# Quantised cross attention: totals and clips on GpSimd, two V roundings on VectorE, weights scaled one row tile later, value products in two visits

## The reference, cut to what matters

```
def _fq(x, delta, zp, n_bits):
    xi = _round_ste(x / delta) + zp
    xq = jnp.clip(xi, 0.0, 2.0 ** n_bits - 1.0)
    return (xq - zp) * delta

k = (ctx @ wk).reshape(b, m, H, DH).transpose(0, 2, 1, 3)
v = (ctx @ wv).reshape(b, m, H, DH).transpose(0, 2, 1, 3)
sim = einsum('bhid,bhjd->bhij', _fq(q, dq, 128.0, 8), _fq(k, dk, 128.0, 8)) * SCALE
attn = softmax(sim, axis=-1)
out = einsum('bhij,bhjd->bhid', _fq(attn, dw, 0.0, 8), _fq(v, dv, 128.0, 8))
```

## Time and profile before

| what | value |
|---|---|
| median of 3 runs | 2426.47 us (2419.76 to 2426.48) |
| the profiled execution | 2418.64 us, of which the span is 2417.0 us |
| mean granted TensorE clock | 0.907 |
| busy share of the span | TensorE 82%, VectorE 71%, ScalarE 56%, GpSimd 29% |
| this stage in the trace | 1675 to 2352 us |

### The profile page before, as it was taken

How to read it: one execution, slowest core, us unless ns; L and a number is a source line. 1 busy time by engine, 2 the same in 40 slices (tenths; PEclk the granted TensorE clock), 3 DMA queues, 4 the chain that set the end, 5 groups by cost and what they waited for, 6 DMA issues and landing times. The chain is left out here.

```text
span 2417.0 us, 58085 instructions
## 1 busy us (share of the span) xinstructions
PE 1986.4 (82%) x19941; PEld 1285.8 (53%) x19941; DVE 1709.3 (71%) x3300; ACT 1360.2 (56%) x2415; POOL 694.8 (29%) x510
## 2 busy tenths in 40 slices
PE   3778677599999999999887785445988888888888
PEld 3778243266666666666534452222555555555553
DVE  3556496677777777777523326995899999999984
ACT  2544243266666666666533333222888888888862
POOL 0000161111111111111000002331766666666630
PEclk8999798799999999999988897556999999999999
DMA  7888000223323323233009980000111111111100
GB/s 193 228 237 222 5 1 0 77 71 91 91 68 95 84 75 95 79 80 95 20 38 280 270 228 1 0 0 26 42 40 35 38 38 38 38 38 38 38 1 15
DMA packets 108285, 190.36 MB, mean 79 GB/s; under 512 B 19886, under 2 KB 75294, under 8 KB 108222
## 3 DMA queue, kind: packets, MB, share of 16 engines
q1 hardware_dynamic: 103614, 164.95, 25.2%
q0 software_dynamic: 4608, 24.58, 3.1%
HBM read 127.13 MB, written 25.49 MB: 63 GB/s over the span
## 5 line engine op out<-in xcount | busy, mean ns | idle before, releaser
L1217 DVE TENSOR_REDUCE c_part<-c_mxp 128x1 f32<-128x500 f32 x672 | 429.4, 674 | 173.7 <-PE c_mxp L1106 169.3
L1190 ACT ACTIVATE c_e<-c_stp 125x896 f32<-125x896 f32 x384 | 351.9, 917 | 97.1 <-PE c_stp L1118 96.5
L1854 ACT ACTIVATE c_e<-c_sp,alpha 128x750 f32<-128x750 f32 x448 | 392.7, 882 | 23.6 <-PE c_sp L1798 21.4
L1812 PE MATMUL c_tp<-ident_h,c_ph 128*128 128x128 f16 x2688 | 230.5, 223 | 72.7 <-DVE c_pt L1874 70.8
L1812 PEld LDWEIGHTS c_tp<-ident_h,c_ph 128*128 128x128 f16 x2688 | 181.1, 100 | 167.7 <-DVE c_pt L1874 113.5
L1106 PE MATMUL c_mxp<-c_kh,c_qb 128*128 128x500 f16 x672 | 254.2, 380 | 3.1 <-DVE c_part L1217 2.2
L1874 DVE TENSOR_SCALAR c_pt<-c_tp 125x768 bf16<-125x768 f16 x448 | 246.3, 550 | 3.5 <-PE c_tp L1812 2.2
L1768 POOL TENSOR_SCALAR c_ki<-c_clipped 128x500 bf16<-128x500 bf16 x96 | 193.0, 2010 | 150.6 <-DVE c_clipped L1885 138.3
L1060 POOL TENSOR_TENSOR c_qs<-qst,mask_quad_ 96x224 f16<-96x224 f32 (+1 forms) x128 | 67.5, 556 | 578.1 <-PE c_stp L1118 578.1
L1133 PE MATMUL c_pvp<-c_e,c_vx 125*32 125x168 f32 (+1 forms) x6144 | 227.0, 265 | 0.6 <-ACT c_e L1190 0.4
L1918 DVE TENSOR_SCALAR c_ph<-c_e,c_inv 128x1500 f16<-128x1500 f32 x224 | 224.1, 1000 | 4.3
(11 more groups left out here) (267 smaller groups left out, 3452.9 us busy)
## 6 DMA issues: line engine op xcount, KB each, us to landing
c_ct<-ctx_turned SPq DMA_DIRECT2D x64, 750.0 KB
ctx_turned<-l_ct POOLq DMA_DIRECT2D x32, 750.0 KB, 4.7
c_ks<-c_kh SPq DMA_DIRECT2D x256, 93.8 KB
f_ct<-ctx_turned SPq DMA_DIRECT2D x32, 750.0 KB
l_cn<-in_ctx SPq DMA_DIRECT2D x32, 672.0 KB
f_cn<-in_ctx SPq DMA_DIRECT2D x32, 672.0 KB
c_ks<-c_kl SPq DMA_DIRECT2D x128, 93.8 KB
l_cn<-in_ctx SPq DMA_DIRECT2D x32, 78.0 KB
```

Of the source, the lines that this page charges most:

```text
L1190: act.activation(e[:, j % 4, :].rearrange("p (a c) -> p a c", a=2), stp[0:KP, 2 * (j % 2):2 * (j % 2) + 2, 0:448], ACT.Exp, scale=SCALE).t ...
L1217: dve.reduce_max(part[:, s // 3, s % 3:s % 3 + 1], mxp[:, (PIECES * p + s) % 2, 0:500], axis=AX.X).then_inc(piece_max, 1)
L1812: last = pe.transpose(tp[:, h, 128 * k:128 * k + 128], ph[r][:, KP * j:KP * j + 128], m.ident_h[:, :])
L1854: act.activation(e[r][:, HALF * h:HALF * h + HALF].rearrange("p (k c) -> p k c", k=2), sp_[:, 2 * h:2 * h + 2, 0:375], ACT.Exp, scale=m.al ...
```

## The change

GpSimd takes the totals, one column per row tile, and the whole clip: first to the limits with ROUND still in the number, in f32 (c_clamped), then ROUND taken off, into bf16. VectorE rounds the pieces 4 and 5 of V from PSUM (ON_VECTOR); ScalarE keeps the other four. VectorE makes the weights of row tile t - 1 in slot t. There are four buffers c_e instead of two, and c_half, c_total and c_inv have a column per row tile. Projections stand in the slots 0, 1, 2, 4, 5, 6 (PROJECT), and the value products in two visits of six steps, in slots 3 and 5 (WEIGH). The turn on TensorE and the copies on VectorE stay in their slots. The diff, cut to its core:

```diff
-        WEIGH = [0, 2, 5, 7, 9, NJ]
+        PROJECT = (0, 1, 2, 4, 5, 6)
+        WEIGH = {3: (0, 6), 5: (6, NJ)}
+        E_BUFFERS = 4
+        ON_VECTOR = (4, 5)
+        USED_BACK = [4 if t >= E_BUFFERS else NT if t == 3 else 3 for t in range(NT)]
-        clipped = pair("clipped", [128, 512], BF16)
+        clamped = pair("clamped", [128, 512])
-        e = pair("e", [128, NK])
+        e = [sb(f"e{t}", [128, NK]) for t in range(E_BUFFERS)]
-        half = sb("half", [128, 2, 2])
-        total, inv = sb("total", [128, 1]), sb("inv", [128, 1])
+        half = sb("half", [128, NT, 2])
+        total, inv = sb("total", [128, NT]), sb("inv", [128, NT])
...
+                def clip(n, p, k, live):
+                    i = 6 * n + k
+                    rows, width = (128, 500) if k < 3 else (KP, 512)
+                    if k >= 2 or live(1):
+                        pool.wait_ge(proj_ready, i - 1)
+                    wait_apart(pool, proj_rounded, i + 1, beat)
+                    pool.tensor_scalar(clamped[k % 2][0:rows, 0:width], rounded[k % 2][0:rows, 0:width],
+                                       ROUND + 127.0, ROUND - 128.0, ALU.min, ALU.max).then_inc(proj_clamped, 1)
...
+                    wait_apart(pool, proj_clamped, i + 1, beat)
+                    pool.tensor_scalar(out, clamped[k % 2][0:rows, 0:width], -ROUND, 1.0, ALU.add, ALU.mult
+                                       ).then_inc(proj_ready, 1)
...
-                        pool.tensor_scalar(out, clipped[t % 2][0:rows, 0:width], -128.0, None, ALU.max
-                                           ).then_inc(proj_ready, 1)
-                sweep(pool, step, 0)
+                    for t in range(NT):
+                        if live(1):
+                            i = NT * (n - 1) + t
+                            wait_apart(pool, exped, 2 * i + 2, beat)
+                            pool.tensor_scalar(total[:, t:t + 1], half[:, t, 0:1], half[:, t, 1:2], m.delta[:, 7:8],
+                                               ALU.add, ALU.mult).then_inc(totalled, 1)
+                        if live(0) and t in PROJECT:
+                            clip(n, p, PROJECT.index(t), live)
+                sweep(pool, step, 1)
...
-                        if 2 <= t and live(2):
-                            for j in range(WEIGH[t - 2], WEIGH[t - 1]):
+                        if t in WEIGH and live(2):
+                            for j in range(*WEIGH[t]):
...
+                            i = NT * (n - 1) + t
+                            if t >= E_BUFFERS or live(2):
+                                act.wait_ge(p_ready, i - USED_BACK[t] + 1)
...
+                def invert(a, t):
+                    i = NT * a + t
+                    dve.wait_ge(totalled, i + 1)
+                    dve.reciprocal(inv[:, t:t + 1], total[:, t:t + 1]).then_inc(inverted, 1)
+
+                def weights(a, t, r, first):
+                    i = NT * a + t
+                    dve.wait_ge(inverted, i + 1)
+                    if t >= 2 or not first:
+                        dve.wait_ge(p_turned, 2 * (i - 1))
+                    dve.tensor_scalar(ph[r][:, 0:NK], e[t % E_BUFFERS][:, :], inv[:, t:t + 1], HALF_ROUND,
+                                      ALU.mult, ALU.add).then_inc(p_ready, 1)
...
+                        if t == 0:
+                            made = live(2)
+                            item = (n - 2, NT - 1)
+                            r, first = (NT * p + NT - 1) % 2, not live(3)
+                        else:
+                            made = live(1)
+                            item = (n - 1, t - 1)
+                            r, first = (NT * (1 - p) + t - 1) % 2, not live(2)
...
+                            if h == 0 and made:
+                                invert(*item)
+                        if made:
+                            weights(*item, r, first)
+                        if live(0) and t in PROJECT and PROJECT.index(t) in ON_VECTOR:
+                            k = PROJECT.index(t)
+                            i = 6 * n + k
+                            dve.wait_ge(proj_done, i + 1)
+                            dve.wait_ge(proj_clamped, i - 1)
+                            dve.tensor_scalar(rounded[k % 2][0:KP, :], pp[0:KP, 0:512], m.rdelta[0:KP, 6:7],
+                                              ROUND, ALU.mult, ALU.add).then_inc(proj_rounded, 1)
```

More of the change, by code:

```diff
@@ L1770, in _ @@
-                sweep(pool, step, 0)
+                def clip(n, p, k, live):
[6 more added lines that the diff above has]
+                                       ROUND + 127.0, ROUND - 128.0, ALU.min, ALU.max).then_inc(proj_clamped, 1)
+                    if k < 3 and live(2):
+                        pool.wait_ge(s_done, 2 * NT * (n - 1))
+                    if k >= 3 and live(2):
+                        pool.wait_ge(weighed, NJ * (n - 2) + 4 * (k - 2))
+                    wait_apart(pool, proj_clamped, i + 1, beat)
+                    out = (ki[p][:, 500 * k:500 * k + 500] if k < 3 else
+                           vi[p][:, 4 * (k - 3):4 * (k - 3) + 4, :].rearrange("p j c -> p (j c)"))
+                    pool.tensor_scalar(out, clamped[k % 2][0:rows, 0:width], -ROUND, 1.0, ALU.add, ALU.mult
+                                       ).then_inc(proj_ready, 1)
@@ L1848, in step @@
                         if live(1):
-                            a, r = n - 1, (NT * (1 - p) + t) % 2
-                            if t >= 2 or live(2):
-                                act.wait_ge(p_ready, NT * a + t - 1)
+                            i = NT * (n - 1) + t
+                            if t >= E_BUFFERS or live(2):
+                                act.wait_ge(p_ready, i - USED_BACK[t] + 1)
                             for h in range(2):
-                                act.wait_ge(s_done, 2 * NT * a + 2 * t + h + 1)
-                                act.activation(e[r][:, HALF * h:HALF * h + HALF].rearrange("p (k c) -> p k c", k=2),
+                                act.wait_ge(s_done, 2 * i + h + 1)
+                                act.activation(e[t % E_BUFFERS][:, HALF * h:HALF * h + HALF]
+                                               .rearrange("p (k c) -> p k c", k=2),
                                                sp_[:, 2 * h:2 * h + 2, 0:375], ACT.Exp, scale=m.alpha[:, 1:2],
-                                               accum_out=half[:, r, h:h + 1]).then_inc(exped, 1)
-                        if live(0) and t < 6:
-                            i = 6 * n + t
+                                               accum_out=half[:, t, h:h + 1]).then_inc(exped, 1)
+                        if live(0) and t in PROJECT and PROJECT.index(t) not in ON_VECTOR:
+                            k = PROJECT.index(t)
+                            i = 6 * n + k
                             act.wait_ge(proj_done, i + 1)
[L1860 to L1863, removed]
+                            if k >= 2 or live(1):
+                                act.wait_ge(proj_clamped, i - 1)
+                            rows, width, d = (128, 500, 5) if k < 3 else (KP, 512, 6)
+                            act.activation(rounded[k % 2][0:rows, 0:width], pp[0:rows, 0:width], ACT.Identity,
                                            bias=m.round[0:rows, 0:1], scale=m.rdelta[0:rows, d:d + 1]
```

45 lines of the change are left out of this document (13 added, 32 removed).

## The result

The changed kernel takes 2485.5 us (median of 4 runs, 2482.5 to 2495.3) against 2423.1 for the kernel before (4 runs): ratio 1.0265, 95% interval 1.023 to 1.030, so 62 us slower. Its profiled execution took 2482.5 with a span of 2480.9, 64 more than the span before. The stage now runs from 1675 to 2415 us, 740 instead of 677: all of the difference lies in it.

What follows compares the result with a forecast made beforehand. VectorE ends last now; after the change, the c_ph-turn-copy chain and GpSimd's exclusion bound it. 11.4 + 2.76 + 3.22 + 4.92 = 22.3, or 20.8; middle 21.5, plus 0.5: 22.0 per item, +47 us, 2468; range 2405 to 2605.

Steps and rivals of the forecast that it cites:

- the main case: Whole kernel: the change makes it slower, 2468 us within 2440 to 2510; chance 0.42.
- The chain: From c_ph over TensorE's turn and VectorE's copies to the next c_ph: 2.76 us a slot, bounds 2.6 and 2.9.
- VectorE's work: Per item VectorE loses 7 totals (2.2) and 6 clips (1.9), gains 2 V roundings (1.2): net -2.9 us.
- GpSimd's pass: c, one clip pass of 500 columns on GpSimd: 0.80 us, ends 0.51 and 1.45; two passes per piece.
- The slot behind slot 5: After VectorE's rounding, GpSimd's passes run from 0.57 to 2.23 and c_ph ends at 3.22 us.
- The boundary: Between items: c_ph ends at 4.92 us if behind GpSimd's c_qb, 3.40 if in front; the middle taken.
- The lower clock: 0.5 us per item above the clean sum, kept from the present item: TensorE waits at the boundary, granted clock 0.92.
- The totals: On GpSimd, one column, 0.17 us each; 1 to 1.5 us of queue hidden while c is below about 1.
- Rival A: GpSimd's pass costs what its present clip does, c = 1.45: 26.3 us an item, 2605 us; chance 0.25.
- Rival B: The chain holds but c_qb falls into a gap: 20.7 us an item, no change, 2430 us; chance 0.10.
- Rival C: As B, with c_total and c_ph not blocked at the boundary and no lower clock: 2414 us; chance 0.15.
- Rival D: Turn and copy never wait for the newest c_ph, TensorE's work decides: 18.4 us an item, 2361 us; chance 0.08.

Runs made afterwards that it cites:

- Opening the chain: Changed kernel with TensorE's turn and VectorE's copies also one slot later (row tile t - 3 in slot t): 2356.6 us, ratio 0.971 to the kernel before.
- form experiment: Changed kernel with the six pieces clipped on GpSimd in six different forms of operations and types, to price them: 2610.6 us, a single execution.

## Why the prediction was right

Forecast 2468, measured 2485.5, inside the 2440 to 2510 of the main case; slower, by 45 forecast and 62 measured. The mechanism is the forecast's: the chain sets the slots and the collision lengthens the boundary. Of its signs, VectorE's busy share fell to 0.80 as it says, and TensorE waits for c_ph; VectorE's wait for turned halves is 135 us where it says 60 to 110, and c_ph's mean 1160 ns where it says 1200 or more. By its own steps:

- The chain. Forecast 2.76 a slot; measured 2.80, and 2.79 in the slot shown above. The one guess in it, the wake-up of 0.04, measured 0.03; the start of the turn came 0.13 after c_ph, not 0.10. Opening the chain gave 129 us, so it is shown as a cause, not only seen.
- VectorE's work. Forecast -2.9 us an item; its busy time fell by 39 us, 1.2 an item, of which the held c_ph take back 1.0 (256.8 us for all c_ph against 224.1 before). A V rounding lasts 0.74 where I took 0.67. The work fell, and did not decide.
- GpSimd's pass. I took c = 0.80 between 0.51 and 1.45; it is 0.61. So the passes do not set the slots after ScalarE's roundings: 2.80, which is the chain, instead of 2.85. To interpolate between a write and c_qb was the wrong way to a price: the form experiment shows neighbours at 0.61, 1.47 and 1.93. It was luck that 0.80 fell near, and the error had a price at the boundary.
- The slot behind slot 5. Forecast 3.22, held by passes; measured 3.06 from c_ph's end to c_ph's end (2002.79 to 2005.85). With two steps of the value products instead of six in slot 5 a pass held c_ph to the same 3.06, so two limits lie together here.
- The boundary. I put c_ph 0.16 behind c_qb and took the middle of both orders, (4.92 + 3.40) / 2 = 4.16. It is 0.34 behind in the item shown, and it is held: 4.71 from c_ph's end to c_ph's end (2005.85 to 2010.56). This is the mis-sized term, 0.55 us an item or 17 in all. With c = 0.61 in the prediction's own sum c_qb would have started 0.55 in front of c_ph instead of 0.16, and there would have been no order left to halve.
- The lower clock. I carried 0.5 over from the kernel before; it is 0.69, worth 6 us. In sixteen of 27 items TensorE's standstill of 2.3 us is followed by slower matmuls, for instance a K projection in 1.98 instead of 1.06 and a slot of 3.53 where the clock is 0.57.
- The totals. Forecast 0.17; alone 0.34, and 0.83 in the median, since most start inside a c_ph. VectorE waited for them 5.1 us only: the queue was hidden, as said.

An item at full clock adds up to 5 x 2.80 + 3.06 + 4.71 = 21.8, and with the 0.69 to the measured 22.45. Against the forecast 22.0 the chain and slot 5 are 0.3 too high, the boundary and the clock 0.7 too low. So the forecast came as near as it did partly because its errors cancel.

Rival A gave 2605 for passes of 1.45. The form experiment, with four of twelve passes at 1.5, four at 1.9 and four at 0.6, took 2611. The number fits, but not by the sum that gave it: there c_ph stands behind the passes, and in the run it is the totals that do and the reciprocal that waits. The prediction names that wait, for c above 1, but gives it no price. Rival B's item, 20.7, is the one of the run with c_qb in slot 3, 20.67, and its 2430 fits the 2435; but it keeps the 0.5 of lower clock, which that run does not have. Rival C has the mechanism of that run, no collision and no lower clock, and is 21 us too low: its slots of 2.76 are 2.80, and its boundary is 3.36 where the run has 3.55 (c_ph's end at 1986.99 to 1990.54). Rival D's item, with the chain open, is (2250.45 - 1752.77) / 27 = 18.43 us, from these rows of the kernel with the later turn, against the 18.4 that I gave it:

```profile
1752.77 1.69 POOL L1776 TENSOR_TENSOR c_qb<-qi,mask_head_ 128x896 bf16<-128x896 f32 x1
...
2250.45 1.69 POOL L1776 TENSOR_TENSOR c_qb<-qi,mask_head_ 128x896 bf16<-128x896 f32 x1
```

## What to carry to other kernels

Moving a step one slot later in one engine's list takes the slack out of every consumer that stays where it was: go round the loop of engines and add it up before you count the work saved. When all busy shares fall and the stage gets longer, look for such a loop, and move the consumer too. A long instruction of an engine that excludes another belongs where the other has nothing of that kind to do; the same move was worth 50 us in a tight order, where it also brought the granted clock back to 1.00, and about 20 in a slack one. When an engine waits, ask which instruction it waits for before naming the cause: slow passes cost their time through a one-column total that queued behind them. And a weight load and its matmul can show one wait twice.

## What the runs showed of the hardware

GpSimd's tensor_scalar on 500 to 512 columns took 0.60 for min with max, 0.61 for add with mult, 1.47 to 1.49 for one operation and 1.92 to 1.93 for subtract with min and max with mult, with no difference between f32 and bf16 where both were tried. A GpSimd total of a single column took 0.34 alone and 0.83 in the median, most of them inside a c_ph. VectorE's total of a single column, in the kernel before, took 0.22 while a GpSimd clip ran (at 2013.86) but 1.65 against a c_qb (at 2022.52). In the changed kernel a c_ph that started 0.34 after a c_qb took 2.15 instead of 0.99. TensorE's standstills of 2.3 us were followed by a granted clock of 0.57 to 0.67 over 4 us in sixteen of 27 items and of 1.00 in eleven.
